# A bias product moved into the free row tile beside three 32-row products, shifts turned in one product, and new step lists for five engines

## The reference

```
x = x + leaky(sum_e gate_e * (gn(x) @ We[e] + be[e]))           # 5 experts, the best 2 by gn(x) @ Wg, softmax
t = tokens(x)                                                   # 16 x 256 tokens
t = t + (softmax(causal(k q^T / sqrt(96))) v) @ wproj + bproj   # 6 heads of 16, k, q, v from ln(t)
h = gelu(ln(t) @ w1[e] + b1[e])                                 # 4 experts, 96 -> 384
y = h @ w2[e] + b2[e]                                           # 384 -> 96
t = t + sum_e masked_e * y_e                                    # the best 2 of 4, softmax over 4
```

## Time and profile before

| what | value |
|---|---|
| median of 3 runs | 316.29 us (316.01 to 317.96) |
| the profiled execution | 316.23 us |
| its span, first to last instruction | 314.5 us |
| busy: PE, DVE, ACT, POOL | 297.0, 238.7, 221.1, 106.3 us |
| mean granted TensorE clock | 0.998 |

### The profile page before, as it was taken

How to read it: one execution, slowest core, us unless ns; L and a number is a source line. 1 busy time by engine, 2 the same in 40 slices (tenths; PEclk the granted TensorE clock), 3 DMA queues, 4 the chain that set the end, 5 groups by cost and what they waited for, 6 DMA issues and landing times.

```text
span 314.5 us, 9387 instructions
## 1 busy us (share of the span) xinstructions
PE 297.0 (94%) x3459; PEld 214.7 (68%) x3459; DVE 238.7 (76%) x1050; ACT 221.1 (70%) x441; POOL 106.3 (34%) x176
## 2 busy tenths in 40 slices
PE   5889899998999999999999999999999999999995
PEld 2655445665656877778677786777686787877774
DVE  4769989997899898898899788799738845813433
ACT  2879778886678997787766495773986769472660
POOL 4444567549821450065070006720622041100000
PEclk9999999999999999999999999999999999999999
DMA  7930054625637010034133003610380111002000
GB/s 178 185 41 0 1 120 72 113 83 125 101 82 115 4 45 0 4 96 113 36 81 95 4 3 77 128 31 14 87 112 3 29 27 44 0 10 62 2 27 25
DMA packets 28436, 18.70 MB, mean 59 GB/s; under 512 B 16820, under 2 KB 26952, under 8 KB 28392
## 3 DMA queue, kind: packets, MB, share of 16 engines
q1 hardware_dynamic: 28392, 18.12, 27.4%
HBM read 3.12 MB, written 1.57 MB: 15 GB/s over the span
## 4 chain that ended last, share of the span: by engine, by line
PE 65%; SPq 2%; DMA 1%; ACT 1%; DVE 1%; issue 1%; POOL 1%; DVEq 0%; POOLq 0%; ACTq 0%
PE PS L1010 21%; PE PS L988 8%; PE PS L989 7%; PE PS L994 4%; PE PS L946 4%; PE PS L961 3%; PE PS L862 3%; PE PS L904 2%; PE PS L928 2%; PE PS L1003 2%; PE PS L854 2%; SPq L509 2%; PE PS L893 1%; DMA k_stack<-qk_parts 1%; PE PS L932 1%; PE PS L975 1%
## 5 line engine op out<-in xcount | busy, mean ns | idle before, releaser
L793 ACT ACTIVATE hidden<-PS,b_t 128x512 f32<-128x512 f32 x96 | 59.5, 683 | 33.1 <-PE PS L994 32.9
L1010 PE MATMUL PS<-w_f,hidden 128*64 128x96 f32 x1536 | 70.4, 248 | 0.0
L1010 PEld LDWEIGHTS PS<-w_f,hidden 128*64 128x64 f32 x1536 | 64.4, 137 | 7.0 <-issue 7.0
L1266 DVE SCALAR_TENSOR_TENSOR res<-PS,weight,res 128x96 f32<-128x96 f32 x128 | 31.4, 309 | 35.5 <-PE PS L1010 35.2
L988 PE MATMUL PS<-t_a,w_a 128*128 128x512 f32 x96 | 42.0, 437 | 0.0
L989 PE MATMUL PS<-t_b,w_b 128*128 128x512 f32 x96 | 37.9, 395 | 0.0
L1170 DVE CUSTOM_DVE_ANT_0 masked<-PS,causal 128x128 bf16<-128x128 f32 (+1 forms) x120 | 34.9, 352 | 3.6 <-PE PS L893 2.1
L769 ACT ACTIVATE prob_a<-PS 128x512 f32<-128x512 f32 x48 | 25.9, 601 | 10.8 <-PE PS L928 10.7
L654 POOL TENSOR_SCALAR_AFFINE_SELECT prob_a<-prob_a 128x768 f32<-128x768 f32 x16 | 13.8, 865 | 57.0 <-ACT prob_a L769 57.0
L1131 DVE SCALAR_TENSOR_TENSOR PS<-conv_y,weight,PS 128x96 f32<-128x96 f32 x128 | 30.2, 316 | 2.5 <-ACT PS L721 2.4
L575 POOL TENSOR_TENSOR ln_var<-ln_mv,eps_t 128x4 f32<-128x4 f32 x16 | 3.2, 198 | 74.6 <-DVE ln_mv L1063 74.6
(11 more groups left out here) (157 smaller groups left out, 613.4 us busy)
## 6 DMA issues: line engine op xcount, KB each, us to landing
q_stack<-qk_parts SPq DMA_DIRECT2D x48, 96.0 KB, 3.2
k_stack<-qk_parts SPq DMA_DIRECT2D x48, 96.0 KB, 3.7
t_c<-t_a SPq DMA_DIRECT2D x24, 64.0 KB, 2.0
out_dram<-res SPq DMA_DIRECT2D x8, 192.0 KB, 2.5
X<-in_x_dram SPq DMA_DIRECT2D x4, 192.0 KB, 2.9
X<-in_x_dram SPq DMA_DIRECT2D x2, 384.0 KB, 5.1
hidden<-in_L_ffn_w_dram SPq DMA_DIRECT2D x1, 576.0 KB
w_f<-in_L_ffn_w_dram SPq DMA_DIRECT2D x1, 576.0 KB
```

The lines of the kernel that those rows point to most:

```text
L793: act.activation(hidden[:, m, 0:T * P], PS[:, bank("ffn1", n, index), 0:T * P], ACT.Gelu, bias=b1_t[:, m:m + 1]).then_inc(act_emptied["ffn ...
L1010: mm = pe.matmul(PS[strip:strip + STRIP, y, t * C:(t + 1) * C], hidden[:, m, t * P + strip:t * P + strip + STRIP], w2_f[:, m, :], start=Fa ...
L1266: ins = dve.scalar_tensor_tensor(res2[:, t, :], PS[:, y, t * C:(t + 1) * C], weight1[:, t, e:e + 1], res2[:, t, :], ALU.mult, ALU.add).the ...
```

## The change

Five things.

First, the second bias. Its three parts now lie in rows 96, 97 and 98 of `b2_parts` (C is 96), and its product reads these three rows alone. These rows are the fourth group of 32. The three 32-row products of expert e+1 are issued by step `ffn2` of expert e just ahead of the bias of expert e; `rest1` remains a step of its own for expert 0 alone. The wait for the Gelus of expert e moves behind the bias. So 24 of 32 `ffn2` steps contain a `rest1`, and expert 3's has the bias alone.

Second, the parts of the bias are made in one partition, and three small DMAs on SP (`w_b2`) place them; a semaphore `b2_placed` takes the place of `b2_split` in ACT's first Gelu and PE's first `ffn2`. Two of the three loads of the bias, two POOL copies and two memsets on DVE go.

Third, the shifts. `shift_parts` has the tile as its last axis, so that one transpose per unit turns all 72 columns; ACT copies 72 rows of 128 instead of 18 rows of 512, and the DMA reads 72 rows of 128.

Fourth, the lists in `ORDER` are new for all engines. PE's has 63 filler products in 8 groups (before 89 in 13), and its shape at the end is `... rest1.0@7 ffn2.3@6 ffn2.0@7 ffn1.6@7 ... ffn1.11@7 ffn2.1@7 ffn2.2@7 ffn2.3@7`, before `... ffn2.0@7 ffn1.9@7 ffn1.10@7 ffn1.11@7 rest1.2@7 rest1.3@7 ffn2.1@7 ffn2.2@7 ffn2.3@7`. On SP, `w_w1.0` moves from behind the shift of unit 0 to behind the stacks of unit 2, where `w_b2`, `w_w1.1` and `t2@0` follow it. In ACT's list the functions Gelu on one side and Exp on the other alternate 22 times, before 18.

Fifth, counts of loads and pads that follow from this.

```diff
 # PE
+            def rest_rows(n, e):
+                T = size_of(n)[1]
+                for j in range(CHUNKS):
+                    rows = slice(j * REST, (j + 1) * REST)
+                    pe.matmul(PS[:, bank("ffn1", n, (e * CHUNKS + j,)), 0:T * P], w1_c[rows, e, :],
+                              t2_cs[n % T2][rows, 0:T * P], start=False, stop=True).then_inc(filled["ffn1"], 1)
...
                 elif kind == "rest1":
-                    e = index[0]
-                    for j in range(CHUNKS):
...
+                    rest_rows(n, 0)
                 elif kind == "ffn2":
                     e = index[0]
                     if n == 0 and e == 0:
-                        pe.wait_ge(b2_split, 3)
-                    wait_act(pe, "ffn1", n, (CHUNKS * (e + 1) - 1,))
+                        pe.wait_ge(b2_placed, 16 * 3)
                     wait_bank_free(pe, "ffn2", n, index)
                     y = bank("ffn2", n, index)
-                    pe.matmul(PS[:, y, 0:T * C], ones_b[:, :],
-                              b2_parts[:, e * C:(e + 1) * C].unsqueeze(1).to_broadcast([P, T, C]),
+                    if e + 1 < E1:
+                        rest_rows(n, e + 1)
+                    pe.matmul(PS[:, y, 0:T * C], ones_b[C:C + 3, :],
+                              b2_parts[C:C + 3, e * C:(e + 1) * C].unsqueeze(1).to_broadcast([3, T, C]),
                               start=True, stop=False, skip_group_check=True)
+                    wait_act(pe, "ffn1", n, (CHUNKS * (e + 1) - 1,))
...
                 elif kind == "shift":
                     wait_bank_free(pe, "shift", n)
                     pe.wait_ge(shift_ready, n + 1)
-                    for t in range(T):
-                        mm = pe.transpose(PS[0:SHIFT * HEADS, bank("shift", n), t * P // 2:(t + 1) * P // 2].bitcast(BF16),
-                                          shift_parts[:, t, :, :].rearrange("p a h -> p (a h)"), ident_b[:, :])
-                    mm.then_inc(filled["shift"], 1)
+                    pe.transpose(PS[0:SHIFT * HEADS * TILES, bank("shift", n), 0:P // 2].bitcast(BF16),
+                                 shift_parts[:, :, :, :].rearrange("p a h t -> p (a h t)"), ident_b[:, :]).then_inc(filled["shift"], 1)
 # ACT
-                    act.activation(shift_t[:, 0:T * P], PS[0:SHIFT * HEADS, bank("shift", n), 0:T * P // 2].bitcast(BF16), ACT.Copy
+                    act.activation(shift_t[:, :], PS[0:SHIFT * HEADS * TILES, bank("shift", n), 0:P // 2].bitcast(BF16), ACT.Copy
 # SP
-                    sp.dma_start(k_stacks[n % 2][STACK:STACK + SHIFT, :, 0:T * P], shift_t[:, 0:T * P]).then_inc(shift_placed, 16)
+                    sp.dma_start(k_stacks[n % 2][STACK:STACK + SHIFT, :, :].rearrange("p h (a t) -> p (h a) t", t=P),
+                                 shift_t[:, :]).then_inc(shift_placed, 16)
...
+                elif kind == "w_b2":
+                    sp.wait_ge(b2_step, 4)
+                    sp.wait_ge(b2_split, 1)
+                    for i, part in enumerate((b2_lead[:, 0, :], b2_lead[:, 1, :], b2_last[:, :])):
+                        sp.dma_start(b2_parts[C + i:C + i + 1, :], part).then_inc(b2_placed, 16)
 # POOL
-                        pool.tensor_copy(b2_parts[0:1, :], b2_lead[0:1, 0, :]).then_inc(b2_split, 1)
-                        pool.wait_ge(b2_split, 1)
-                        pool.tensor_copy(b2_parts[32:33, :], b2_lead[32:33, 1, :]).then_inc(b2_split, 1)
-                        pool.wait_ge(b2_split, 2)
-                        pool.tensor_copy(b2_parts[64:65, :], b2_rest[64:65, 1, :]).then_inc(b2_split, 1)
-                        pool.wait_ge(b2_split, 3)
+                        pool.tensor_copy(b2_last[:, :], b2_rest[:, 1, :]).then_inc(b2_split, 1)
```

More of the change, by code:

```diff
@@ L62 @@
[L62 to L66, removed]
@@ new lines @@
+        norm1_t@2 xn@5 qk.0@2 qk.1@2 prob.0.0@0 prob.0.1@0 prob.0.2@0 prob.0.3@0 prob.0.4@0 prob.1.0@0 prob.1.1@0
+        prob.1.2@0 prob.1.3@0 prob.1.4@0 shift@1 tanh@4 leaky@3 xn@6 conv.0@5 v@1 conv.1@5 conv.2@5 prob.0.0@1
+        prob.0.1@1 prob.0.2@1 v@2 prob.0.3@1 prob.0.4@1 prob.1.0@1 prob.1.1@1 prob.1.2@1 prob.1.3@1 prob.1.4@1 norm2@0
+        norm2_t@0 norm1@3 conv.3@5 norm1_t@3 xn@7 qk.0@3 qk.1@3 mix@4 ffn1.0@0 ffn1.1@0 ffn1.2@0 ffn1.3@0 ffn1.4@0
+        gexp@0 shift@2 ffn1.5@0 tanh@5 ffn1.6@0 ffn1.7@0 ffn1.8@0 norm2@1 leaky@4 ffn1.9@0 ffn1.10@0 ffn1.11@0 mix@5
@@ new lines @@
+        v@3 norm2_t@1 prob.0.0@2 prob.0.1@2 prob.0.2@2 prob.0.3@2 norm1@4 prob.0.4@2 prob.1.0@2 conv.0@6 conv.1@6
+        conv.2@6 conv.3@6 norm1_t@4 prob.1.1@2 gexp@1 prob.1.2@2 prob.1.3@2 prob.1.4@2 qk.0@4 qk.1@4 ffn1.0@1 ffn1.1@1
+        ffn1.2@1 ffn1.3@1 ffn1.4@1 ffn1.5@1 leaky@5 tanh@6 shift@3 ffn1.6@1 ffn1.7@1 mix@6 ffn1.8@1 norm2@2 ffn1.9@1
+        ffn1.10@1 ffn1.11@1 norm2_t@2 prob.0.0@3 prob.0.1@3 prob.0.2@3 prob.0.3@3 prob.0.4@3 prob.1.0@3 prob.1.1@3
+        prob.1.2@3 prob.1.3@3 prob.1.4@3 leaky@6 gexp@2 norm1@5 conv.0@7 conv.1@7 conv.2@7 v@4 norm1_t@5 conv.3@7
@@ new lines @@
+        qk.0@5 qk.1@5 ffn1.0@2 ffn1.1@2 ffn1.2@2 tanh@7 ffn1.3@2 ffn1.4@2 ffn1.5@2 norm2@3 mix@7 norm2_t@3 ffn1.6@2
+        ffn1.7@2 ffn1.8@2 norm1@6 ffn1.9@2 ffn1.10@2 ffn1.11@2 shift@4 norm1_t@6 ffn1.0@3 ffn1.1@3 ffn1.2@3 prob.0.0@4
+        prob.0.1@4 prob.0.2@4 prob.0.3@4 prob.0.4@4 prob.1.0@4 prob.1.1@4 prob.1.2@4 prob.1.3@4 prob.1.4@4 qk.0@6
+        shift@5 gexp@3 qk.1@6 ffn1.3@3 ffn1.4@3 ffn1.5@3 ffn1.6@3 ffn1.7@3 leaky@7 ffn1.8@3 ffn1.9@3 ffn1.10@3
+        ffn1.11@3 prob.0.0@5 prob.0.1@5 prob.0.2@5 prob.0.3@5 prob.0.4@5 prob.1.0@5 prob.1.1@5 norm2@4 v@5 v@6
@@ new lines @@
+        score.1.3@1 score.1.4@1 shift@1 mix.4@3 qk.1@2 gates.1@4 att.0@0 att.1@0 proj@0 xadd@3 stats1@3 score.0.0@2
+        score.0.1@2 score.0.2@2 score.0.3@2 score.0.4@2 score.1.0@2 score.1.1@2 score.1.2@2 norm2_t@0 score.1.3@2
+        w_gate@0 att.0@1 att.1@1 qk.0@3 score.1.4@2 qk.1@3 mix.1@4 gates.0@5 shift@2 gate2@0 mix.2@4 proj@1 weights@0
+        mix.3@4 mix.4@4 ffn2.0@0 xadd@4 ffn2.1@0 gates.1@5 ffn2.2@0 stats1@4 mix.1@5 norm2_t@1 score.0.0@3 ffn2.3@0
+        mix.2@5 score.0.1@3 score.0.2@3 mix.3@5 score.0.3@3 gate2@1 score.0.4@3 score.1.0@3 score.1.1@3 score.1.2@3
@@ new lines @@
+        score.1.0@5 score.1.1@5 score.1.2@5 score.1.3@5 score.1.4@5 shift@5 gate2@3 ffn2.3@2 weights@3 qk.0@6 qk.1@6
+        mix.4@7 att.0@4 att.1@4 ffn2.0@3 ffn2.1@3 ffn2.2@3 proj@4 score.0.0@6 score.0.1@6 score.0.2@6 score.0.3@6
+        score.0.4@6 xadd@7 score.1.0@6 score.1.1@6 stats1@7 ffn2.3@3 score.1.2@6 score.1.3@6 norm2_t@4 att.0@5
+        score.1.4@6 att.1@5 shift@6 gate2@4 proj@5 weights@4 qk.0@7 qk.1@7 ffn2.0@4 ffn2.1@4 norm2_t@5 gate2@5 ffn2.2@4
+        score.0.0@7 score.0.1@7 score.0.2@7 score.0.3@7 score.0.4@7 score.1.0@7 score.1.1@7 score.1.2@7 score.1.3@7
@@ L172 @@
+        prob.0.0@7 prob.0.1@7 prob.1.0@7 prob.1.1@7 rstd2@7
         """,
     SYNC: """
[L174 to L177 removed]
@@ L179 @@
+        stk.5@6 t2@4 store@2 store@3 shift@6 stk.0@7 stk.2@7 stk.4@7 stk.1@7 stk.3@7 stk.5@7 t2@5 shift@7 t2@6 store@4
         t2@7 store@5 store@6 store@7
```

229 lines of the change are left out of this document (100 added, 129 removed).

## The result

The changed kernel takes 312.81 us (median of 5 runs, 311.3 to 314.97) against 316.01 us of the kernel before on the same chip (5 runs, 315.55 to 317.96): ratio 0.9881, 95% interval 0.9839 to 0.9924. That is some 3.8 us faster, where 9.8 were forecast. Its profiled execution is its fastest, 311.3 us with a span of 309.6.

The account below looks back on a forecast made before the run. Bound: a chain with DVE nearly full to 92 us, PE with DVE close behind to 225, then PE alone. 7.3 + 1.2 - 0.5 + 1.4 + 2.5 - 2.0 = 9.9 us off 316.2: 306.3, given as 306.5; range 301.2 to 314.

Parts of the forecast that it names:

- the lists made anew: First stage, before the first FFN product: fillers fall from 89 to 63, 2.5 us gained (ends 0 and 5.6).
- the new wait: Second products, where PE waits for its expert's Gelus right after the bias: 2 us lost (bounds 0 and 16.3).
- The bias beside the rest: Second products: the bias hides beside the next expert's three 32-row products, 27 x 0.27 = 7.3 us gained.
- Fewer tile-shape changes: Full-width product behind a trio: its shape change is saved, 0.05 us at 24 places, 1.2 us gained.
- five lone biases: Biases not beside a trio change the shape from 128 rows to 32: 5 x 0.1 = 0.5 us lost.
- Shifts: Score shifts on PE: one transpose instead of four spares 0.17 us, 8 x 0.17 = 1.4 us gained.
- Bias set-up: Loads, memsets, copies and three small DMAs on SP: room just used up, 0, at most 0.4 us lost.
- the Gelu wait: Rival: at 24 second products, waiting for Gelus takes the place of the bias; slower, 320.6 us; chance 0.10.
- the fourth tile run in series: Rival: the bias runs after the three 32-row products, 1.1 us gained instead of 7.3; 312.5 us; chance 0.12.
- Everything lands: Rival: whole kernel, no friction and all left-out fillers are real idle time; 301.2 us; chance 0.14.
- DVE holds the pace: Rival: up to 225 us DVE sets the pace, about half of PE's 9.4 us is lost; 313.5 us; chance 0.14.
- a clock below 1.00 before 92 us: Sign of a wrong forecast: in the first stage the granted clock falls below 1.00, since fewer fillers run there.

Follow-up runs that it names:

- old_shift: Kernel before with one part of the change alone, the score shifts turned in one product: 314.00 us, ratio 0.9938 to the kernel before.
- joint_wide: Changed kernel's code in the order of the kernel before, 15 biases hidden, the 17 lone biases over 128 rows: 311.36 us, ratio 0.9854 to the kernel before.
- bias_full: Changed kernel with the bias product over all 128 rows again, so it can't run beside the trio: 318.03 us, ratio 1.0023 to the kernel before.
- before_less: Kernel before with 26 of its 89 filler products left out: 317.09 us, ratio 1.0024 to the kernel before.
- tanh_first: Changed kernel with one word of ACT's list moved, tanh@3 ahead of qk.0@1: 313.41 us, ratio 0.9869 to the kernel before.
- tanh_fill: Changed kernel with tanh@3 moved ahead of qk.0@1 in ACT's list and 23 fillers put back early: 313.44 us, ratio 0.9883 to the kernel before.
- old_joint: Changed kernel's code in the lists of the kernel before, every rest its own step, 15 biases hidden, lone ones three rows: 311.71 us, ratio 0.9848.
- fill: Changed kernel with 23 fillers put back in six places of PE's early list: 311.73 us, ratio 0.9864 to the kernel before.

## Why the prediction was wrong

The direction was right and the time within the range, but the gain was about 0.4 of the forecast. The step that failed first is "the lists made anew", with its companion "the new wait": 0.5 us gained was forecast, 2.7 us were lost. The other is a size: the hidden biases were counted whole, and three to four fifths of them arrived.

- **The bias beside the rest** (7.3 us forecast): the mechanism and the price on PE are right, 27 x 0.27. Taken alone it is worth 4.5 us by ratio (2.8 to 6.1 with both intervals) and 5.7 in the late stage of the trace; the old order gives the same kind of share, 2.7 us by ratio and 2.6 in the late stage for 15 x 0.27 = 4.1 (old_shift to joint_wide). The rest of each 0.27 us doesn't arrive; that PE then waits a little more on others fits the waits by starts (in bias_full DVE's part is 4.6 us, after 5.2) but accounts for less than half of it.
- **Fewer tile-shape changes, five lone biases** (1.2 and -0.5): a lone small bias costs 0.1 us in the rows shown, as forecast. The first term was not run by itself. In the trace of the kernel before, the instructions behind a trio hold PE 1.3 us longer in all than the same instructions elsewhere, so the forecast's 1.2 was there to be spared on PE.
- **Shifts** (1.4): 2.0 us by ratio, since one transpose holds PE 0.08 us and not the 0.16 that were left in the forecast (0.33 less 0.17).
- **Bias set-up** (0): nothing waits for it. The three parts have landed by 86.2 us in the trace, and the first Gelu starts at 96.2.
- **The lists made anew** (+2.5): this step failed. It took fillers left out as time given back. before_less shows that 26 fewer give no time that can be seen, and the clock fell in it. The new early order was no shorter either: DVE waited 1.9 us for a tanh that ACT's list had put behind a wait for a transfer, which tanh_first and tanh_fill show to be worth 1.3 to 1.4 us of that stage. Instead of 2.5 us gained, 0.9 were lost; with that one word mended the stage is as long as before (87.94 against 88.27, less than two executions of one kernel differ), still with two falls of the clock.
- **The new wait** (-2.0, at the Gelus): its place was wrong, and its size 3.5 us (6.2 less 2.7 by starts). PE waits for no Gelu ahead of a second product; ACT's 22 table loads are there, and in 21 of them the next activation starts within 0.02 us. PE waits 4.4 us more for DVE, with DVE no fuller than before. The prediction read DVE's 14.5 us of idle time as room. What counts is when DVE's list reaches the instruction that empties a bank, and the new lists changed that order.

By ratios the change is the sum of three: the shift 2.0 us gained (old_shift), the new order with its fewer fillers 2.7 us lost (old_shift to bias_full, 0.0085; roughly 1.2 to 4.2 with both intervals), the 27 hidden biases 4.5 us gained (bias_full to after, 0.0142). The forecast had 1.4, 0.5 gained (2.5 less 2.0) and 8.0 (with the tile shapes and the lone biases). The 2.7 is not the clock's alone: in the two traces the same step costs 2.8 us, and 2.1 of them lie in the late stage (220.49 to 222.54), where both ran at 1.00. The late stage of the changed kernel adds up within half a microsecond: 7.3 + 1.2 - 0.5 and 6 shifts x 0.25 = 1.5 spared on PE, 3.5 of new waits, which leaves 6.0; measured 5.5.

Of the rivals, the Gelu wait and the fourth tile run in series are refuted, and that the second of them gave 312.5 us, almost the time measured, is chance. "Everything lands" is refuted by the time. "DVE holds the pace" gave 313.5 us, near the time measured too, but by DVE's load: DVE has no more to do than in old_joint, where PE's waits for it are not there, which points to the handover. The prediction's sign for a wrong outcome, a clock below 1.00 before 92 us, came true. What it cost is not told apart from the early order: putting fillers back (fill) won 0.5 us by the ratio and 1.1 by the medians, inside the interval.

What stays open: how much of each run's time the clock takes, since it falls in other places from run to run (four runs of fill with a mean clock of 0.994 took 311.5 to 311.9 us, the two at 0.989 and 0.984 took 313.9 and 313.8); and why a fifth (by the traces) to two fifths (by the ratios) of each hidden bias's 0.27 us is missing.

## What to carry to other kernels

Here a product that runs in a free row tile beside three others cost PE nothing, but with step lists in a fixed order the time came only as far as the order of the others was kept: fifteen hidden biases in the old order were worth as much as twenty-seven in a new one, and three more, bought by moving three second products, cost 8.7 us, some of it by a fall of the clock. Don't count fillers left out as time, and don't read an engine's idle share as room: look for which instruction stands behind a wait in each list (here a ready tanh behind a transfer) and who empties the bank that PE needs next. Test a change of instructions and a change of order separately, since here one gained what the other gave back.

## What the runs showed of the hardware

The granted clock fell to one half (1.2 GHz) within a stage in which PE was far from idle. The changed kernel and the kernel before in the same two stretches:

```profile
47.00:53.90 6.90, 4.33 (x33) 2.31 (x32) 5.00 (x20) 5.22 (x15) 2.61 (x4) 1.00 0.32 74
53.90:60.70 6.80, 5.56 (x17) 4.11 (x16) 6.70 (x21) 2.89 (x7) 4.16 (x8) 0.50 0.60 106
```

```profile
47.00:53.90 6.90, 6.38 (x59) 3.71 (x57) 6.42 (x28) 5.55 (x15) 4.59 (x10) 1.00 0.46 70
53.90:60.70 6.80, 6.47 (x40) 4.48 (x37) 6.70 (x20) 6.30 (x15) 5.14 (x5) 1.00 0.73 133
```

After, PE was busy 4.33 of the 6.90 us ahead of the fall; before, with fillers, 6.38, and the clock stayed. But it also fell behind a stretch with PE busy 8.49 of 9.00 us, in tanh_fill:

```profile
107.00:116.00 9.00, 8.49 (x137) 7.08 (x133) 8.10 (x45) 8.50 (x18) 2.38 (x5) 1.00 0.23 57
116.00:122.80 6.80, 6.80 (x22) 5.42 (x22) 3.88 (x22) 3.85 (x8) 0.86 (x1) 0.50 0.02 5
```

Nothing in these rows tells why it fell there: the changed kernel runs the same steps at 1.00. Such a fall in the stage where PE sets the end costs nearly half its length: tanh_fill's late stage, with 6.8 us at the half clock, is 2.9 us longer than tanh_first's, and fill's, with 3.4 us, is 1.5 us longer than the changed kernel's.
